# Second buffers and other PSUM banks behind the experts, and another order of loads and folds at the start, in a two-layer vision-text kernel

## The chip, the cores and the metric

One core of a Trainium2 chip runs the whole program, all of it in float32. The metric is the time of one execution on the device in microseconds; several executions of a kernel are timed, and their median is its time.

## The reference, cut to what matters

16 samples of 96 tokens (64 image patches and 32 text tokens) of 192 features pass through a patch embedding and two layers.

```python
x: (16, 3, 128, 128)   txt: (16, 32, 192)
# 1. patch tokens: the image and four shifted copies, cut into 16x16 patches (3840 values),
#    normalised and projected; folded here into 768 inner + 192 halo values a patch
tn = (t - mu) * rsqrt(var + 1e-05) * ln_weight + ln_bias
tok = einsum('bnk,dk->bnd', tn, proj_weight) + proj_bias
h = concatenate([tok, txt], 1)                        # (16, 96, 192)
# 2. layer 0: attention over 4 segments of 24 tokens, 12 heads; then top-2 of 8 experts
h += attention0(layernorm(h))
h += moe(layernorm(h))        # capacity 60 slots a pair group, F = 768, relu
# 3. layer 1: linear attention with L1-normalised q and k
q, k, v = split(layernorm(h) @ w_qkv.T)
q, k = q / sum_n |q|, k / sum_n |k|                   # over the tokens of a sample
h += (q @ (k^T @ v by head of 16)) @ w_proj.T + b_proj
# 4. layer 1: soft mixture, 8 experts x 4 slots
logits = l2norm(layernorm(h)) @ (scale * l2norm(slots))
xs = softmax(logits, over tokens)^T @ x ; y = expert_mlp(xs) with gelu
h += softmax(logits, over slots) @ y
```

## The kernel before

**Tiling.** The 1536 tokens lie in J = 4 tiles j of four samples. A tile is `h[:, j]`: 128 partitions (32 tokens of each of the four samples) by NB = 3 blocks by 192 features; blocks 0 and 1 are image tokens, block 2 is text. Every engine has its own program, written out by hand as a list of calls at the end of its block (TensorE lines 887 to 1142, ScalarE 1309 to 1450, VectorE 1900 to 2081, GpSimd 418 to 477, SyncE 294 to 349). Semaphores named in `wait_ge`, `need` and `free` tie them together; what stands behind a waiting call on the same engine waits too. PSUM has eight banks of 512 float32 a partition, given out by hand in constants (`TOK_AT`, lines 77 to 80) and by number inside the functions.

**Start.** SyncE issues all early loads (294 to 325): layernorm weights, the projection weights in four chunks (`load_weights`, 31 tiles of 128 x 192), the constants, images as eight pairs (`load_images`, 271: 448 KB of inner values and 32 KB of halo on 64 partitions, into NX = 6 places), the text tokens, then the weights of the first attention (316 to 323) and last images 4 to 7. VectorE folds the 31 weight tiles into KT = 8 tiles `w_eff` (`fold_weights`, 1463): for tile t a multiplication and up to four multiply-adds into the same destination, each of which waits for the one before it through `then` (1458); `head_values` (1547) later waits for the attention's weights. TensorE sums bias and columns (`weight_sums`, 499; the first WIDE_TILES = 15 bias matmuls are 128 columns wide, the others 32 wide on four column groups in turn) and multiplies patches (`patch_tile`, 490: four matmuls of 32 rows out, one for each sample; tile t = 7 has only 64 rows of contraction). `patches(2, 0)` (542, called at 896) waits for images 4 and 5. `scores(0)` (622) writes banks 5 to 7. ScalarE squares each image pair (`squares`, 1150); squares of images 6 and 7 (1318, 1319) stand ahead of `keep_inputs(0)` (1322), which copies the turned inputs that `reduce_inputs(0)` (595) needs. VectorE's `token_rows` (1492) reads what a patch matmul left.

**Experts.** `expert_inner` and `expert_outer` (702, 724) are a run of matmuls from 129 to 260 us. For the tiles j = 2 and 3, GpSimd gathers the experts' rows from DRAM (`fetch_row`, 446: 12 gathers) between its powers for the layernorms (`norm_scale`, 413), and VectorE adds them (`add_rows`, 1758); for j = 0 and 1 TensorE combines them (`combine`, 746; `add_experts`, 1749).

**Behind the experts** each tile passes through these steps. `linear_norm` (1775, VectorE) writes `xn`; `turn_linear` (764, TensorE) turns it with `flip` (246) into banks 0 and 1: 96 of its features would fill 96 rows twice, so it takes 128 features and 64 features instead, and the 64 are turned to two places so that the matmuls of 64 rows can use either half of the array. `linear_queries` (785) has two full matmuls and two of 64 rows, one on each half; `linear_keys_values` (774) writes banks 2 to 4, one full and one 64-row matmul a block, those of blocks 0 and 1 on different halves. ScalarE copies (`keep_linear_inputs` 1258, `keep_keys_values` 1264, `keep_linear_queries` 1271, `keep_linear_outputs` 1276). `key_products` (795) multiplies k and v into banks 1 to 4; `own_heads` (1811, VectorE) masks the product; `key_sums` (806), `key_norms` (1780), `query_norms` (1787), `norm_products` (1795) and `scale_queries` (1804) make the L1 norms; `linear_outputs` (813) and `linear_project` (823) end the attention, `add_linear` (1818) adds it. The soft layer follows: `soft_moments` and `soft_norm` (1827, 1834), `turn_soft`, `soft_logits`, `soft_max`, `slot_weights` (1858), `soft_inputs` (854, TensorE, bank 7), `keep_slots`, and for three tiles together and the last alone `soft_hidden` (862), `gelu_slots` (1303), `keep_own` (1880), then `slot_outputs` (870), `add_up_bias`, `token_outputs` (877) and `add_soft` (1892). One buffer each of `xn`, `xs`, `xsT`, `o1T`, `dsp_bd`, `mv_b`, `rs_b`, `mv_s` and `soft_st` serves all tiles.

```python
            def linear_queries(j):
                pe.wait_ge(sem("b_xnT"), j + 1)
                for mh in range(2):
                    nc.tensor.matmul(PS[0:HD, mh, 0:TOK], w_q1[:, 0, mh * HD:(mh + 1) * HD], xnT[:, 0], start=True, stop=False)
                for mh in range(2):
                    rows = slice(mh * DT, (mh + 1) * DT)
                    mm = nc.tensor.matmul(PS[0:HD, mh, 0:TOK], w_q1[rows, 1, mh * HD:(mh + 1) * HD], xnT[rows, 1],
                                          start=False, stop=True)
```

## Time and profile before

| | |
|---|---|
| median of 3 runs | 366.97 us (364.63 to 372.05) |
| profiled execution | 366.12 us, of which the span of instructions is 364.0 us |
| mean granted TensorE clock | 0.986 of full speed |
| busy, share of the span | TensorE 325.9 us (90%), VectorE 195.5 (54%), ScalarE 112.1 (31%), GpSimd 52.1 (14%) |
| HBM traffic | 19.94 MB read, 2.75 MB written |

The span runs from the first to the last instruction; 2.1 us of the execution lie around it. A float32 matmul shows in the trace as two matmul instructions, so "x4" in a row stands for two matmuls. Busy times of TensorE are modelled at their ends and overlap a little. "Released by" or "<-" names what ended a wait. The granted clock is 1.00 at TensorE's full clock (2.4 GHz) and half of that at the lower level (1.2 GHz).

### The profile page before, as it was taken

The numbers are of one execution on the slowest core, as the hardware profiler recorded it, in microseconds if no ns is written. First come the engines' busy times: TensorE is split into PE (matmuls) and PEld (weight loads), VectorE is DVE, ScalarE is ACT, GpSimd is POOL, SyncE is SP. The second block draws the span as 40 slices with busy tenths as digits, with TensorE's granted clock in tenths as the row PEclk, the third lists the DMA queues.
The fourth block names the chain that finished last, engine by engine and source line by source line (L and its number), as shares of the span: only waits on it lengthen the run. The fifth ranks groups of instructions, "written<-read, shape, count | busy, mean of one in ns | idle before, by whom it ended". The sixth has DMA issues, their size and how long they took to land.

```text
span 364.0 us, 9315 instructions
## 1 busy us (share of the span) xinstructions
PE 325.9 (90%) x3978; PEld 216.6 (60%) x3978; DVE 195.5 (54%) x636; ACT 112.1 (31%) x218; POOL 52.1 (14%) x99
## 2 busy tenths in 40 slices
PE   4898999887788989999999999999987899997765
PEld 3675567655665337475656657475854556666455
DVE  2925497899999971142312111120367655968655
ACT  1224444665642431404041221203012213333140
POOL 8403222100011000000010000000087201100100
PEclk9999999999999999999999999999999989999889
DMA  7936011332030000504132240000012000000005
GB/s 266 346 85 220 2 38 31 117 125 96 19 105 1 2 0 2 151 17 137 50 103 74 81 137 16 23 2 22 24 54 67 13 0 0 3 2 2 0 0 130
DMA packets 15876, 23.29 MB, mean 64 GB/s; under 512 B 3770, under 2 KB 11932, under 8 KB 15836
## 3 DMA queue, kind: packets, MB, share of 16 engines
q1 hardware_dynamic: 14364, 20.93, 18.4%
q0 software_dynamic: 576, 1.18, 1.2%
q10 hardware_dynamic: 896, 0.59, 0.7%
q8 instruction: 31, 0.51, 0.6%
q14 instruction: 9, 0.07, 0.1%
HBM read 19.94 MB, written 2.75 MB: 62 GB/s over the span
## 4 chain that ended last, share of the span: by engine, by line
PE 61%; DVE 20%; SPq 7%; issue 4%; DMA 3%; POOL 2%; ACT 2%; DVEq 0%; POOLq 0%; ACTq 0%
PE banks L719 18%; PE banks L734 17%; SPq L320 4%; PE banks L496 3%; PE banks L249 3%; PE banks L778 2%; PE banks L858 2%; DVE sb_onehot_combT L1695 2%; PE banks L820 2%; PE banks L830 2%; PE banks L788 2%; DMA sb_tok_xeT<-in_xhalo 2%; DVE sb_stat L1517 1%; POOL sb_onehot_combT L455 1%; PE banks L782 1%
## 5 line engine op out<-in xcount | busy, mean ns | idle before, releaser
L719 PE MATMUL banks<-sb_tok_xeT,sb_wi_sl 128*128 128x480 f32 (+1 forms) x192 | 64.9, 590 | 1.1 <-ACT sb_tok_xeT L1236 1.1
L734 PE MATMUL banks<-sb_wo_sl,sb_attn_hidT_attn 128*60 128x192 f32 x768 | 64.1, 327 | 0.0
L734 PEld LDWEIGHTS banks<-sb_wo_sl,sb_attn_hidT_attn 128*60 128x60 f32 x768 | 52.9, 133 | 12.4 <-issue 4.0
L1251 ACT ACTIVATE sb_attn_hidT_attn<-banks 128x480 f32<-128x480 f32 x48 | 25.6, 569 | 95.7 <-PE banks L719 95.7
L719 PEld LDWEIGHTS banks<-sb_tok_xeT,sb_wi_sl 128*128 128x128 f32 (+1 forms) x192 | 24.9, 187 | 37.7 <-issue 35.8
L1743 DVE COPY sb_w_tok_e_out<-banks 60x384 f32<-60x384 f32 x16 | 8.9, 555 | 61.9 <-PE banks L734 61.6
L496 PE MATMUL banks<-sb_tok_xeT 128*32 128x193 f32 (+1 forms) x512 | 24.7, 328 | 1.5 <-DMA sb_tok_xeT<-in_xhalo 1.5
L496 PEld LDWEIGHTS banks<-sb_tok_xeT 128*32 128x32 f32 (+1 forms) x512 | 17.2, 109 | 7.2 <-issue 4.5
L1745 DVE COPY sb_onehot_combT<-banks 60x384 f32<-60x384 f32 x16 | 8.9, 555 | 22.1 <-PE banks L734 22.0
L618 PE MATMUL banks<-sb_w_v,sb_xrT 97*32 97x96 f32 x512 | 13.7, 249 | 1.8 <-issue 1.2
L1155 ACT ACTIVATE sb_onehot_combT<-sb_tok_xeT 128x1024 f32<-128x1024 f32 x8 | 8.5, 1058 | 19.3 <-DMA sb_tok_xeT<-in_xhalo 19.0
L1517 DVE BATCH_NORM_STATS2 sb_stat<-sb_h 128x6 f32<-128x192 f32 x48 | 14.1, 348 | 0.5
L858 PE MATMUL banks<-sb_attn_hidT_attn 128*96 128x128 f32 x48 | 8.8, 353 | 5.7 <-DVE sb_attn_hidT_attn L1865 5.7
L618 PEld LDWEIGHTS banks<-sb_w_v,sb_xrT 97*32 97x32 f32 x512 | 10.8, 110 | 5.2 <-issue 2.1
L455 POOL DMA_INDIRECT sb_onehot_combT<-expert_rows,sb_row_of x12 | 12.1, 1011 | 6.6 <-DMA expert_rows<-sb_onehot_combT 3.4
L508 PE MATMUL banks<-sb_w_tok_e_out,sb_ln_b 128*128 128x192 f32 x30 | 7.7, 421 | 5.2 <-DMA sb_w_tok_e_out<-in_wtok 5.2
L443 POOL TENSOR_TENSOR sb_soft_stat<-sb_soft_stat,sb_half 128x6 f32<-128x6 f32 x4 | 5.3, 1337 | 47.4 <-DVE sb_soft_stat L1832 47.4
L1730 DVE TENSOR_TENSOR sb_comb<-sb_cst,sb_slot_of 128x480 f32<-128x480 f32 x6 | 3.9, 654 | 15.0 <-PE banks L249 15.0
L778 PE MATMUL banks<-sb_w_kv,sb_xnT 128*128 128x384 f32 x24 | 9.9, 520 | 1.9 <-DVE sb_attn_hidT_attn L1815 1.6
L858 PEld LDWEIGHTS banks<-sb_attn_hidT_attn 128*96 128x96 f32 x48 | 7.7, 221 | 6.4 <-DVE sb_attn_hidT_attn L1865 6.4
L438 POOL MEMSET sb_attn_hidT_attn<- 1x384 f32 x1 | 0.4, 412 | 77.0 <-PE banks L734 77.0
L249 PE MATMUL banks<-sb_cst,sb_attn_hidT_attn 128*128 128x128 f32 (+1 forms) x72 | 10.4, 278 | 0.7 <-DVE sb_attn_hidT_attn L1577 0.7
(252 smaller groups left out, 537.6 us busy)
## 6 DMA issues: line engine op xcount, KB each, us to landing
sb_wo_sl<-in_wo SPq DMA_DIRECT2D x8, 576.0 KB, 4.5
sb_tok_xeT<-in_xin SPq DMA_DIRECT2D x8, 448.0 KB, 5.4
sb_wi_sl<-in_wi SPq DMA_DIRECT2D x8, 288.0 KB, 3.0
sb_wi_sl<-in_wi SPq DMA_DIRECT2D x24, 96.0 KB, 3.0
sb_w_tok_e_out<-in_wtok SPq DMA_DIRECT2D x2, 960.0 KB, 7.5
expert_rows<-sb_onehot_combT SPq DMA_DIRECT2D x8, 192.0 KB, 4.2
sb_w_tok_e_out<-in_wtok SPq DMA_DIRECT2D x1, 576.0 KB, 9.5
out<-sb_h SPq DMA_DIRECT2D x8, 72.0 KB, 2.0
```

Source lines behind the costliest of these rows:

```text
L249: return nc.tensor.transpose(dst, src, ident[0:rows, 0:rows])
L320: sp.dma_start(dst, src).then_inc(sem("attn0_in"), 16)
L455: gp.indirect_dma_start(rows_in[:, i], None, expert_rows, bass.IndirectOffsetOnAxis(ap=row_of[:, i:i + 1], axis=0)).then_inc(sem(f"rows_in ...
L496: nc.tensor.matmul(PS[QB * b:QB * b + QB, bank, at:at + D + 1], x_k[0:rows, (2 * j + b // 2) % NX, t, cols], w_eff[0:rows, t], start=(t == ...
L618: mm = nc.tensor.matmul(PS[32 * r:32 * r + 32, V_BANK[b % 2], s * C1:(s + 1) * C1], xrT[:, at:at + 32], w_v4[:, r], start=True, stop=True)
L719: mm = nc.tensor.matmul(PS[:, banks[z], 0:SLOTS], lhs, rhs.rearrange("k g c -> k (g c)"), start=first, stop=not first)
L734: mm = nc.tensor.matmul(PS[64 * z:64 * z + CAP, 4 + hf, pr * D:(pr + 1) * D], hidT[:, e % 2, f, g * CAP:(g + 1) * CAP], wo_sl[:, q, f], st ...
L778: nc.tensor.matmul(PS[:, 2 + blk, 0:2 * D], xnT[:, 0, blk * 128:(blk + 1) * 128], w_kv1[:, 0], start=True, stop=False)
L858: mm = nc.tensor.matmul(PS[0:HD, 7, dh * 128:(dh + 1) * 128], xs[:, blk, dh * HD:(dh + 1) * HD], dsp_bd[:, blk].rearrange("t q s -> t (q s ...
L1251: nc.scalar.activation(hidT[:, e % 2, f], PS[:, HID_BANKS[(e * (FT // 2) + f // 2) % 2][f % 2], 0:SLOTS], ACT.Relu).then_inc(sem("hidT"), 1)
L1517: ve.bn_stats(stat6[:, blk], h[:, j, blk]).then_inc(sem("stat6"), 1)
L1743: ve.tensor_copy(e_out[64 * (e % 2):64 * (e % 2) + CAP, z:z + 3:2, e // 2], src).then_inc(sem("e_out"), 1)
```

## The change

*The start.* The constants are loaded in two parts, the 136 columns that the first work needs early and the rest behind the projection weights. Images 4 and 5 are loaded ahead of the text tokens and the attention's weights. The halo of every image is loaded twice, onto partitions 0 to 63 and 64 to 127; so are the last weight tile and two columns of `ln_w`. With them the last patch tile (t = 7) of the two blocks is done as eight matmuls one after another, block 0 on the upper and block 1 on the lower rows, for j = 0, 1, 2 (`PAIRED`). VectorE folds in the groups `FOLDS` = (0), (1, 2), (3, 4), (5, 6, 7), one shift of each tile in turn. TensorE works in three `STAGES`; WIDE_TILES is 20. Patch tiles of j = 1 and 2 write two banks each, (6, 7) and (4, 5), and `scores(0)` waits for `tok_mid` and `tok_var` of 6 instead of 4.

*Behind the experts.* `xn`, `xs`, `xsT`, `o1T`, `dsp_bd` and the small statistics have a second buffer, in `x_space` or beside the first. `xnT` holds 96 rows twice; `features` is gone, `w_q1` and `w_kv1` hold 96 rows, and layer 1 has 9 loads instead of 15. Queries are four matmuls of 96 rows, keys and values two a block, turning six transposes. Banks are named in constants. The lists of calls of all engines from `combine` on have a new order.

```diff
-WIDE_TILES = 15
+WIDE_TILES = 20
-LAYER1_DMAS = 15
+LAYER1_DMAS = 9
-TOK_AT = (((4, 0), (5, 0)), ((6, 0), (6, 200)), ((4, 0), (4, 200)), ((4, 0), (4, 200)))
+TOK_AT = (((4, 0), (5, 0)), ((6, 0), (7, 0)), ((4, 0), (5, 0)), ((4, 0), (4, 200)))
+FOLDS = ((0,), (1, 2), (3, 4), (5, 6, 7))
+STAGES = (((0, 1, 2), 25), ((3, 4), 25), ((5, 6), W_TILES))
+PAIRED = 3
+COMB_BANKS = ((0, 3), (3, 4))
+LIN_T_BANKS, LIN_Q_BANKS, LIN_KV_BANKS = (0, 1), (1, 3), (1, 0, 4)
+PROD_BANK, SUM_BANK, LIN_O_BANKS, PROJ_BANKS = 4, 0, (1, 2), (3, 2)
+SOFT_T_BANKS, SOFT_LOG_BANK, SOFT_IN_BANK, SOFT_HID_BANKS = (6, 4), 5, 2, (0, 1)
+SLOT_Y_BANKS, TOKEN_Y_BANKS = (6, 3), ((2, 6), (1, 0))
@@ SyncE
-                sp.dma_start(x_k[0:HALO2, q, KT - 1], xhalo[n]).then_inc(sem(f"x_in{q}"), 16)
+                for z in range(2):
+                    sp.dma_start(x_k[HALO2 * z:HALO2 * z + HALO2, q, KT - 1], xhalo[n]).then_inc(sem(f"x_in{q}"), 16)
-            sp.dma_start(cst[:], consts).then_inc(sem("cst_in"), 16)
+            sp.dma_start(cst[:, 0:FIRST_W], consts[:, 0:FIRST_W]).then_inc(sem("ones_in"), 16)
...
+            sp.dma_start(cst[:, FIRST_W:], consts[:, FIRST_W:]).then_inc(sem("cst_in"), 16)
             load_images(2)
             load_images(3)
+            load_images(4)
+            load_images(5)
             sp.dma_start(h[:, :, 2], txt.rearrange("(j b) t d -> (b t) j d", j=J)).then_inc(sem("txt_in"), 16)
...
-            for n in range(4, 8):
+            for n in range(6, 8):
                 load_images(n)
@@ GpSimd
             fetch_row(2, 2, 0)
-            norm_scale("b", 1, rs_b[:], mv_b)
             fetch_row(2, 2, 1)
+            norm_scale("b", 1, rs_b[:, 1], mv_b[:, 1])
             fetch_row(3, 0, 0)
             fetch_row(3, 0, 1)
             fetch_row(3, 1, 0)
+            norm_scale("b", 2, rs_b[:, 0], mv_b[:, 0])
             fetch_row(3, 1, 1)
@@ TensorE
+                if j < PAIRED and blk == 1:
+                    for both in range(2):
+                        patch_tile(j, both, KT - 1)
...
             def linear_queries(j):
                 pe.wait_ge(sem("b_xnT"), j + 1)
                 for mh in range(2):
-                    nc.tensor.matmul(PS[0:HD, mh, 0:TOK], w_q1[:, 0, mh * HD:(mh + 1) * HD], xnT[:, 0], start=True, stop=False)
-                for mh in range(2):
-                    rows = slice(mh * DT, (mh + 1) * DT)
-                    mm = nc.tensor.matmul(PS[0:HD, mh, 0:TOK], w_q1[rows, 1, mh * HD:(mh + 1) * HD], xnT[rows, 1],
-                                          start=False, stop=True)
+                    for kh in range(2):
+                        mm = nc.tensor.matmul(PS[0:HD, LIN_Q_BANKS[mh], 0:TOK], w_q1[:, kh, mh * HD:(mh + 1) * HD], xnT[:, kh],
+                                              start=(kh == 0), stop=(kh == 1))
...
-            free(tok_mid=4, tok_var=4)
+            free(tok_mid=6, tok_var=6)
             scores(0)
-            free(tok_mid=6, tok_var=6)
...
             combine(0, 0)
             combine(0, 1)
+            free(moe_h=2)
             combine(1, 0)
             combine(1, 1)
             turn_linear(0)
             free(b_xnT=1)
+            linear_keys_values(0, 0)
+            linear_keys_values(0, 1)
+            free(b_kv=1, moe_h=3)
             linear_queries(0)
-            linear_keys_values(0, (0, 1))
             free(moe_h=4)
-            linear_keys_values(0, (2,))
-            free(b_q1T=1)
+            linear_keys_values(0, 2)
+            free(b_kv=2, b_q1T=1)
             turn_linear(1)
-            free(b_kv=3, b_xnT=2)
+            free(b_kv=3)
             key_products(0)
+            free(b_xnT=2)
             key_sums(0)
-            free(b_kvbd=1)
-            linear_keys_values(1, (0, 1))
-            linear_keys_values(1, (2,))
+            linear_keys_values(1, 0)
+            free(b_knorm=1)
+            linear_keys_values(1, 1)
             free(b_kv=4)
             linear_outputs(0)
-            free(b_kv=6, b_o1T=1)
+            linear_keys_values(1, 2)
+            free(b_o1T=1)
+            linear_queries(1)
+            free(b_kv=6)
             key_products(1)
...
+            token_outputs(1)
+            free(y_added=2)
             slot_outputs(2)
@@ VectorE, fold_weights
+                for tiles in FOLDS:
+                    for s, t in [(s, t) for s in range(5) for t in tiles if s < len(shifts[t])]:
...
+                        if s == 0:
+                            ins = ve.tensor_scalar(dst, src, scale, None, ALU.mult)
+                        else:
+                            ve.wait_ge(sem("w_fold"), at[t])
+                            ins = ve.scalar_tensor_tensor(dst, src, scale, dst, ALU.mult, ALU.add)
@@ VectorE, the list near its end
+            token_weights(1)
             soft_max(2)
             token_shift(2)
-            add_linear(3, 1)
+            soft_norm(3)
             slot_weights(2)
-            soft_moments(3)
             token_weights(2)
-            soft_norm(3)
             soft_max(3)
```

## Rows read from the trace of the kernel before

**Rows 1.** Busy time by stage: us, each engine's busy (x instructions), clock, DMA share, GB/s.
```profile
0.00:50.00 50.00, 41.44 (x794) 29.68 (x797) 26.79 (x89) 16.90 (x25) 19.47 (x56) 1.00 0.50 168
50.00:268.00 218.00, 207.41 (x2564) 133.48 (x2556) 104.87 (x326) 69.85 (x141) 14.04 (x24) 1.00 0.19 58
268.00:290.00 22.00, 17.70 (x170) 10.36 (x170) 16.22 (x52) 5.87 (x10) 13.25 (x16) 1.00 0.17 46
290.00:331.00 41.00, 36.90 (x309) 24.52 (x310) 27.82 (x101) 11.82 (x24) 4.03 (x3) 0.96 0.00 1
331.00:361.00 30.00, 22.49 (x152) 18.56 (x150) 19.80 (x72) 7.68 (x19) 1.32 (x1) 0.89 0.09 23
```

**Rows 2.** Timeline of TensorE, first 50 us: start us, us, instruction, [idle before].
```profile
12.47 1.89 PE L508 MATMUL banks<-sb_w_tok_e_out,sb_ln_b 128*128 128x192 f32 x10
...
16.13 0.35 PE L523 MATMUL banks<-sb_tok_xeT,sb_cst 128*32 128x192 f32 x1 [1.00 <-DVE sb_tok_xeT L1476]
...
22.48 3.86 PE L496 MATMUL banks<-sb_tok_xeT 64*32 64x193 f32 x78
...
33.59 2.96 PE L496 MATMUL banks<-sb_tok_xeT 128*32 128x193 f32 x64 [1.51 <-DMA sb_tok_xeT<-in_xhalo]
...
46.57 1.32 PE L630 MATMUL banks<-sb_attn_hidT_attn,sb_qT 32*32 32x96 f32 x96 [0.37 <-ACT sb_attn_hidT_attn L1198]
```

**Rows 3.** Timeline of VectorE, first 50 us: folds, and instructions that don't wait.
```profile
10.18 1.79 DVE L1476 SCALAR_TENSOR_TENSOR sb_tok_xeT<-sb_w_tok_e_out,sb_ln_w,sb_tok_xeT 128x192 f32<-128x192 f32 x4
...
29.15 0.41 DVE L1500 SCALAR_TENSOR_TENSOR sb_tok_mid<-sb_col_sum,sb_tok_stat,banks 128x192 f32<-128x192 f32 x1
29.48 0.15 DVE L1503 SCALAR_TENSOR_TENSOR sb_tok_stat<-banks,sb_tok_stat 128x1 f32<-128x1 f32 x1
```

**Rows 4.** Timeline of SyncE's queue (DMA issues), first 60 us.
```profile
15.66 7.47 SPq L320 DMA_DIRECT2D sb_w_px<-in_wproj  x1
...
25.10 0.85 SPq L322 DMA_DIRECT2D sb_w_qkv<-in_bqkv  x1
```

**Rows 5.** Groups by line on TensorE, 268 to 331: busy us, mean ns | idle before.
```profile
L778 PE MATMUL banks<-sb_w_kv,sb_xnT 128*128 128x384 f32 x24 | 9.9, 520 | 1.9 <-DVE sb_attn_hidT_attn L1815 1.6 <-ACT sb_xnT L1262 0.3
L788 PE MATMUL banks<-sb_xnT,sb_w_q 128*96 128x384 f32 x16 | 7.4, 591 | 2.1 <-ACT sb_xnT L1262 1.0 <-DVE sb_attn_hidT_attn L1815 0.6 <-ACT sb_attn_hidT_attn L1279 0.4
...
L801 PE MATMUL banks<-sb_attn_hidT_attn 32*96 32x96 f32 x192 | 5.1, 249 | 1.9 <-issue 1.9
```

**Rows 6.** The chain that ended last, 265 to 364: one piece of it.
```profile
273.01 4.02 DMA sb_onehot_combT<-expert_rows,sb_row_of
```

**Rows 7.** Timeline of ScalarE, first 50 us.
```profile
35.87 1.06 ACT L1155 ACTIVATE sb_onehot_combT<-sb_tok_xeT 128x1024 f32<-128x1024 f32 x1
37.70 0.79 ACT L1173 COPY sb_xnT<-banks 96x768 f32<-96x768 f32 x1 [0.77 <-PE banks L249]
```

**Rows 8.** Timeline of TensorE, 260 to 364.
```profile
270.38 1.50 PE L788 MATMUL banks<-sb_xnT,sb_w_q 128*96 128x384 f32 x4 [1.03 <-ACT sb_xnT L1262]
...
272.63 1.56 PE L778 MATMUL banks<-sb_w_kv,sb_xnT 128*128 128x384 f32 x4
274.12 0.92 PE L782 MATMUL banks<-sb_w_kv,sb_xnT 64*128 64x384 f32 x4
...
276.65 1.20 PE L249 MATMUL banks<-sb_cst,sb_xn 128*128 128x128 f32 x9
...
285.47 1.60 PE L820 MATMUL banks<-sb_attn_hidT_attn 96*96 96x96 f32 x16
...
290.34 2.87 PE L788 MATMUL banks<-sb_xnT,sb_w_q 128*96 128x384 f32 x4 [0.63 <-DVE sb_attn_hidT_attn L1815]
...
330.73 1.57 PE L820 MATMUL banks<-sb_attn_hidT_attn 96*96 96x96 f32 x16 [0.90 <-DVE sb_attn_hidT_attn L1809]
...
348.87 2.88 PE L858 MATMUL banks<-sb_attn_hidT_attn 128*96 128x128 f32 x12 [2.43 <-DVE sb_attn_hidT_attn L1865]
```

**Rows 9.** Timeline of VectorE, 258 to 364: its last instruction.
```profile
360.31 0.35 DVE L1898 TENSOR_TENSOR sb_h<-sb_h,banks 128x192 f32<-128x192 f32 x1
```

446 lines of the change are left out of this document (224 added, 222 removed).

## The prediction

> **What bounds the kernel now.** I read the stages first [rows 1]: the reader is to see that TensorE is busy 207 of 218 us between 50 and 268, and that the time it loses lies in the first 50 us (41.4 busy) and behind the experts: 17.7 of 22, then 36.9 of 41 with the granted clock at 0.96, then 22.5 of 30 at 0.89. VectorE is busy 64 of these last 93 us, so no engine is full there. The change touches only those two ends. Then the start, engine by engine. TensorE waits 1.00 us for a folded weight tile, runs densely from 16.1, and stands idle 1.51 us ahead of the patches of images 4 and 5 [rows 2]. The folds come 0.445 us apart (four in 1.79, each of them 0.42 long and 0.03 of hand-over), though VectorE starts an instruction that doesn't wait 0.33 us after the one in front, 29.15 to 29.48 [rows 3]. SyncE issues the loads of images 4 to 7 late because one small load held it 7.47 us [rows 4]. Last, the layer behind the experts, where the groups of matmuls name the waits [rows 5]: 8.7 us of idle time from 268 to 331 over the view's twelve groups (the three with most of it are shown), behind ScalarE's copies and VectorE's masked products. A part of it hangs on a gather that takes 4.02 us to land [rows 6], behind which VectorE's queue stands.
>
> **The start.** The constants are cut in two and the first weights therefore come some 0.5 us earlier (an estimate: 220 of 288 KB no longer stand ahead of them). *Folds in turns.* 24 dependent folds at 0.445; with a fold of another tile between, the wait is met before it is reached. I take 0.33 a fold for the eight of each pair and 0.445 for the last tile's four: tiles 1 and 2 done near 12.0, 3 and 4 near 15.8, all near 19.0 instead of 20.6. *TensorE.* Five more bias matmuls are 128 columns wide and no longer run four abreast: ten instructions take 1.89 us [rows 2], about 1.4 us more than narrow ones. Against that it needs no fold before it has done 25 bias tiles, so it runs without a gap from 5.25: bias tiles to 15.4, patch tiles 0 to 2 to 17.9, 3 and 4 to 19.5, 5 and 6 to 21.7. *Last tile side by side.* Eight matmuls of 64 rows use both halves of the array at once: 0.37 us saved for each of three pairs, worth 1.1 us in all (0 if they don't run together). The 78 instructions that end at 26.3 [rows 2] thus end near 24.9: 1.4 us gained. *Images moved up.* Images 4 and 5 then land near 23, far ahead of the need at 30.7, so the 1.51 us go and patches(2, 0) ends about 3.2 us earlier.
> What is late next is SyncE's queue. The attention weights are issued behind six more image DMAs, and wherever the queue fills up the 7.47 us come again, now from a later point. By the order of the queue I put the last weight's issue at 29.8 (25.1 to 25.95 before) and its landing near 33; head_values and first_norm(0) wait a few tenths. ScalarE must square images 6 and 7 before it may copy the turned inputs; image 7's square began at 35.87 and the copy at 37.70 [rows 7]. Image 7 was last in the queue before and still is; two images instead of four share the way, so I take 35.3 to 36.3 for its landing and 37.4 for the copy's start at the latest. reduce_inputs(0) comes at 38.0 instead of 40.4: 2.4 us gained. One new wait takes some back: patch tiles of j=2 now lie in banks 4 and 5, so scores(0) waits for VectorE's token rows of tile 5, some 0.4 us beyond the ScalarE copy that released it at 46.57 [rows 2]; behind it in TensorE's queue stand all values(0, ·), and VectorE's score_max waits for it. **The start gains 2.0 us less hops: 1.8.** From there on the attention is a chain over VectorE and TensorE that nothing in the diff touches, and the experts are pure matmul [rows 1], so I carry 1.8 through unchanged. Bounds: 3.2 if only the images count; for the other end see the SyncE rival.
>
> **The layer behind the experts: what it costs TensorE.** The 64-row halves that ran side by side are given up. Queries: two full matmuls (1.50) and two halves together, 2.25 us from 270.38 to 272.63; now four full ones at 0.75, 3.05. Keys and values: 4.02 us from 272.63 to 276.65; now six full ones, 4.6. Turning: six transposes instead of nine (1.20 for nine), about 0.3 us less [rows 8]. Net +1.05 us a tile (0.8 + 0.6 - 0.35), **+4.2 us for four tiles**. The Trainium skill says the same against this edit (TensorEngine Tiling (Array Packing), Key Properties and Theoretical Speedup): tiles on different rows execute in parallel, up to twice as fast with a contraction of 64. The trace agrees, 0.92 us for a pair of 64-row matmuls against 1.56 for two full ones [rows 8]. By a clean factor of two the price would be 1.5 - 0.35 a tile, 4.6 us, and the sum 359.2.
>
> **And what it frees.** combine(1, 0) reuses bank 3 and waits for add_experts(0, 1), 0.4 us. The turned inputs and q, kv no longer share banks 0 and 1 with each other's readers, the four product banks lie apart from kv (4 to 7, against 1 to 4), xn, xs, xsT, o1T, the slot weights and the moments have second buffers, and the kv and query matmuls stand where TensorE waited for VectorE. I walked the three queues with the durations of this trace. Per tile TensorE then has 0.7 turning, 4.6 kv, 3.05 queries, 1.25 products, 0.1 sums, 1.5 outputs, 2.1 projection: 13.3 us, plus 2 to 3.3 us of the soft layer from the third tile on. Starts of linear_outputs: 283.1, 296.4, 310.9, 323.8, against 285.47 (first) to 330.73 (fourth) [rows 8]. Up to there 2.4 us of idle time are left of the 8.7, and the queries at half clock (2.87 against 1.50) become warm, because TensorE has no gap ahead of them; one soft_inputs (1.3) has moved behind. 6.9 us gained there. The gather costs less than it did: POOL issues (2, 2, 1) ahead of the second pow, 1.1 us earlier, but (3, 1, 1) and on now stand behind norm_scale of tile 2; VectorE waits about 0.8 us for them at a place where TensorE has work.
> Behind that comes latency. In VectorE's queue soft_norm(3) stands in front of slot_weights(2), which makes soft_inputs(2) start at 336.2, and soft_logits(3) queues behind it. I keep half clock for the 336 to 343 stretch, as at 348.87 (2.88 for twelve instructions). soft_inputs(3) starts near 343 instead of 348.87, the closing slot and token matmuls take about 0.5 us more (slot_outputs(2) now waits for two additions). Last addition 353.4 instead of 360.3 to 360.7 [rows 9]: 7.3 us. A walk leaves out hand-overs of 0.05 us between engines; for some 35 of them I take 1.8 us off. **The layer gains 5.5 us.** Bounds of this part: minus 4.2 (only the dearer matmuls, no wait gone) and plus 11 (all 8.7 idle, all cold surplus of 331 to 361 gone, less 4.2 and the tail's latency).
>
> **Sum.** 366.12 (profiled execution, span 364.0, 2.1 us around it) - 1.8 - 5.5 = 358.8. The three runs shown had their median at 366.97, 0.85 above the profiled one and within their own scatter of 7 us; I forecast 358.8. A measurement of this kernel tells about 2% from no change, that is 7.3 us: a median under 359.6 is faster.
>
> **Rivals.**
> *Waits only change places.* In-order VectorE still decides in 268 to 331 (27.8 of 41 busy, and each long copy comes with a semaphore hop), so filling matmuls only lengthen the queue ahead of the urgent ones. For it: ScalarE and VectorE idle little when TensorE does. Against: the idle time stands before banks that the change splits. Of 6.9 gained, 4.2 + 1.5 are lost: 366.12 - 1.8 - 0 to 1.5 = 363.5. Chance 0.22.
> *TensorE stays warm to the end.* The half-clock rows of 338 to 352 become full-clock: two soft_inputs 1.4 us less each, the hidden matmuls 1.4, and fewer hops than I took off: 366.12 - 1.8 - 10 = 354.3. For it: the new order has the last soft matmuls close together. Against: 4 to 5 us of idle time ahead of them remain in my walk. Chance 0.17.
> *SyncE pays twice (slower side).* The place is the issue of w_px behind the small packets of v_mask. If it stalls behind the images' queue as well as behind v_mask, another 7.5 us, image 7 lands at 43.4 and its square ends at 44.5; the input copy starts there, 6.8 us later than at 37.70. It decides from the moment that square ends after about 39.5, and with 5.5 gained behind the experts the sum is 366.12 + 6.8 + 0.4 - 5.5 = 367.8; with the first rival too, 371. Chance 0.07.
> *Folds gain nothing.* If VectorE's next instruction can't start before the pipe is empty, folds in turns still come 0.445 apart; all are done at 20.4, and TensorE waits 0.9 us: 359.7. Chance 0.06. The Trainium skill states this (VectorE: DVE Perf Modes, The DRAIN you can't avoid): a semaphore after each operation costs nothing extra. The trace does not agree, 0.33 against 0.445.
> The forecast itself has 0.48, with 356.5 to 361.5 as its own range.
>
> **Chances.** Faster by over 2%: all of the warm case, two thirds of my own, little of the folds: 0.52. Within 2%: 0.42. Slower: 0.06, mostly a stall larger than the one priced. Range 353 to 366: the warm case's middle is inside, the first rival too, the double stall is left out.
>
> **What would show it.** Right: no idle time before the patches of images 4 and 5; folds 0.33 apart; queries of 3.0 us and kv of 1.5 a block; four linear_outputs starts 13 to 14.5 us apart, the first about 4 us, the fourth about 8 to 9 us earlier than now; clock 1.00 in 290 to 300. Wrong: ScalarE's copy of the turned inputs after 38, an idle TensorE over 4 us in 268 to 331, or a clock above 0.95 in the last 30 us.

## The result: 352.6 us, 13 us less than before

The changed kernel takes 352.63 us (median of 4 executions, 350.76 to 353.82) against 365.80 for the kernel before beside it (364.00 to 372.05): ratio 0.965, 95% interval 0.960 to 0.970. The forecast was 358.8 with a range from 353 to 366; the result lies 0.4 us below the range. The direction was right, the size was not: the medians differ by 13.2 us. Between the profiled executions, on which the sum was made, it is 366.12 to 351.75, 14.4 us where 7.3 were forecast. The span is 349.9.

First the stages, to be laid beside [rows 1]. The limits are set at the same places of the program: until the experts' results are being combined, until some 5 us behind the first linear_outputs, until the fourth one, until the last addition. Columns: stretch and its length, busy time of TensorE, its weight loads, VectorE, ScalarE and GpSimd (with instructions), TensorE's granted clock, DMA share, GB/s.

```profile
0.00:50.00 50.00, 42.15 (x850) 30.72 (x850) 26.79 (x95) 18.25 (x28) 18.97 (x56) 1.00 0.57 179
50.00:265.00 215.00, 204.09 (x2496) 131.16 (x2494) 101.89 (x319) 68.49 (x137) 14.27 (x24) 1.00 0.20 57
265.00:285.00 20.00, 18.18 (x131) 11.46 (x126) 16.33 (x52) 6.04 (x10) 13.15 (x17) 1.00 0.19 50
285.00:318.00 33.00, 32.61 (x335) 24.33 (x334) 26.58 (x93) 11.01 (x21) 4.07 (x4) 1.00 0.01 2
318.00:347.00 29.00, 22.45 (x164) 18.94 (x164) 22.02 (x81) 8.68 (x22) 1.90 (x2) 0.94 0.09 24
```

The reader is to see where the gain lies: the third and fourth stretch last 53 us together instead of 63, and TensorE's idle time in them is 2.2 us (53 less 18.18 and 32.61) instead of 8.4. In the last stretch little changed; it is still a quarter idle.

The timeline of TensorE over one tile of the layer, to be laid beside [rows 8] (start us, length us, instruction, count, idle time before it and what ended it):

```profile
265.76 0.86 PE L264 MATMUL banks<-sb_cst,sb_xn 128*96 128x128 f32 x6
267.65 2.82 PE L810 MATMUL banks<-sb_w_kv,sb_xnT 96*128 96x384 f32 x8 [1.03 <-ACT sb_xnT L1290]
270.30 2.74 PE L818 MATMUL banks<-sb_xnT,sb_w_q 96*96 96x384 f32 x8
272.88 1.45 PE L810 MATMUL banks<-sb_w_kv,sb_xnT 96*128 96x384 f32 x4
...
280.21 1.57 PE L847 MATMUL banks<-sb_attn_hidT_attn 96*96 96x96 f32 x16
...
292.42 1.52 PE L847 MATMUL banks<-sb_attn_hidT_attn 96*96 96x96 f32 x16
...
305.90 1.52 PE L847 MATMUL banks<-sb_attn_hidT_attn 96*96 96x96 f32 x16
...
318.02 1.57 PE L847 MATMUL banks<-sb_attn_hidT_attn 96*96 96x96 f32 x16 [0.40 <-DVE sb_attn_hidT_attn L1843]
```

Queries are the eight instructions of L818: from their start to that of the next group, 270.30 to 272.88, it is 2.6 us. Keys and values are the x8 and the x4 of L810, 2.65 and 1.3 us by their starts, 3.95 together. The forecast had 3.05 and 4.6. The four linear_outputs (L847) stand 12.2, 13.5 and 12.1 us apart, where the walk had 13.3, 14.5 and 12.9: about one microsecond less in each. Counted from the start of combine (257.18 now, 259.81 before), the fourth starts at 60.8 instead of 70.9.

At the start, beside [rows 2, 4 and 7], on TensorE, SyncE's queue and ScalarE:

```profile
12.88 1.89 PE L530 MATMUL banks<-sb_w_tok_e_out,sb_ln_b 128*128 128x192 f32 x10 [0.33 <-DMA sb_w_tok_e_out<-in_wtok]
...
37.85 1.51 PE L634 MATMUL banks<-sb_xnT,sb_w_red 96*104 96x384 f32 x4 [0.89 <-ACT sb_xnT L1201]
...
44.44 1.32 PE L666 MATMUL banks<-sb_attn_hidT_attn,sb_qT 32*32 32x96 f32 x96 [0.83 <-DVE sb_tok_stat L1537]
```

```profile
23.32 3.48 SPq L340 DMA_DIRECT2D sb_w_px<-in_wproj  x1
...
28.00 0.85 SPq L342 DMA_DIRECT2D sb_w_qkv<-in_bqkv  x1
```

```profile
35.97 1.06 ACT L1183 ACTIVATE sb_onehot_combT<-sb_tok_xeT 128x1024 f32<-128x1024 f32 x1 [1.02 <-DMA sb_tok_xeT<-in_xhalo]
36.93 0.77 ACT L1201 COPY sb_xnT<-banks 96x768 f32<-96x768 f32 x1
```

The idle time ahead of the patches of images 4 and 5 is gone, SyncE's stall is 3.48 us instead of 7.47, and scores(0) starts at 44.44 instead of 46.57: 2.1 us, forecast 2.0. (Whether the edits earn these 2.1 us is another question; further executions of the old start, below, reach the same place without them.) The last image's square is now directly ahead of the copy, which waits for nothing else.

### The profile page after: what moved, and what is told of

Read it like the earlier page. It is cut to its first block, busy times and chain, and to the rows that moved or that the text cites. A ratio compares the mean times of both kernels' runs of the same rounds, so it can differ in the third digit from the quotient of the medians.

```text
span 349.9 us, 9294 instructions
## 1 busy us (share of the span) xinstructions
PE 319.5 (91%) x3966; PEld 216.6 (62%) x3966; DVE 193.6 (55%) x636; ACT 112.5 (32%) x218; POOL 52.4 (15%) x100
## 4 chain that ended last, share of the span: by engine, by line
PE 64%; DVE 16%; SPq 8%; issue 4%; DMA 3%; POOL 2%; ACT 2%; DVEq 0%; POOLq 0%
PE banks L755 18%; PE banks L770 18%; PE banks L810 3%; PE banks L264 3%; SPq L288 2%; PE banks L818 2%; SPq L340 2%; PE banks L654 2%; PE banks L857 2%; PE banks L847 2%; PE banks L522 2%; DVE sb_onehot_combT L1729 2%; DVE sb_stat L1551 2%; POOL sb_onehot_combT L478 2%; SPq L286 1%
## 5 line engine op out<-in xcount | busy, mean ns | idle before, releaser
L522 PE MATMUL banks<-sb_tok_xeT 128*32 128x193 f32 (+1 forms) x512 | 23.4, 328 | 0.0
L522 PEld LDWEIGHTS banks<-sb_tok_xeT 128*32 128x32 f32 (+1 forms) x512 | 15.8, 109 | 5.9 <-issue 2.3
L810 PE MATMUL banks<-sb_w_kv,sb_xnT 96*128 96x384 f32 x48 | 17.6, 497 | 1.0 <-ACT sb_xnT L1290 1.0
L1551 DVE BATCH_NORM_STATS2 sb_stat<-sb_h 128x6 f32<-128x192 f32 x48 | 14.1, 349 | 0.6
L530 PE MATMUL banks<-sb_w_tok_e_out,sb_ln_b 128*128 128x192 f32 x40 | 8.9, 385 | 5.8 <-DMA sb_w_tok_e_out<-in_wtok 5.8
L478 POOL DMA_INDIRECT sb_onehot_combT<-expert_rows,sb_row_of x12 | 12.3, 1025 | 6.0 <-issue 3.0
L530 PEld LDWEIGHTS banks<-sb_w_tok_e_out,sb_ln_b 128*128 128x128 f32 x40 | 7.9, 225 | 6.6 <-issue 5.4
L810 PEld LDWEIGHTS banks<-sb_w_kv,sb_xnT 96*128 96x128 f32 x48 | 8.5, 190 | 5.4 <-ACT sb_xnT L1290 1.3
L818 PE MATMUL banks<-sb_xnT,sb_w_q 96*96 96x384 f32 x32 | 11.0, 486 | 0.0
L717 PE MATMUL banks<-sb_onehot_combT,sb_xn 64*128 64x480 f32 x48 | 10.7, 578 | 0.2 <-issue 0.2
```

What stands on the lines that cost most here:

```text
L478: gp.indirect_dma_start(rows_in[:, i], None, expert_rows, bass.IndirectOffsetOnAxis(ap=row_of[:, i:i + 1], axis=0)).then_inc(sem(f"rows_in ...
L522: nc.tensor.matmul(PS[QB * b:QB * b + QB, bank, at:at + D + 1], x_k[rows, (2 * j + b // 2) % NX, t, cols], w_eff[rows, t], start=(t == 0), ...
L530: nc.tensor.matmul(PS[:, 0, 0:D], ln_b[:, k:k + 1].to_broadcast([128, 128]), w_tok[:, k], start=(k == 0), stop=False)
L717: mm = nc.tensor.matmul(PS[:, banks[hf], 0:E * CAP], xn2[rows, j, blk, 0:128], onehot[rows, j % 2, blk], start=(blk == 0), stop=(blk == NB ...
L810: mm = nc.tensor.matmul(PS[:, LIN_KV_BANKS[blk], 0:2 * D], xnT[:, kh, blk * 128:(blk + 1) * 128], w_kv1[:, kh], start=(kh == 0), stop=(kh ...
L818: mm = nc.tensor.matmul(PS[0:HD, LIN_Q_BANKS[mh], 0:TOK], w_q1[:, kh, mh * HD:(mh + 1) * HD], xnT[:, kh], start=(kh == 0), stop=(kh == 1))
```

## The experiments

Sixteen kernels ran in four groups, each group beside the kernel before on the same chip (the second and the fourth group on one chip, the others on two more). That kernel's median moved with the chip: 365.1, 371.2, 366.5 and 371.8 us. So times of different groups are compared by their ratio to it only. The last four columns are places in the one profiled execution of each kernel: the starts of scores(0) and of combine, and, counted from the start of combine, the starts of the fourth linear_outputs ("LO4") and of the last addition ("end").

| kernel | median us | ratio to before (95%) | scores(0) | combine | LO4 | end |
|---|---|---|---|---|---|---|
| before | 365.80 | 1 | 46.57 | 259.81 | 70.9 | 100.5 |
| after | 352.63 | 0.965 (0.960 to 0.970) | 44.44 | 257.18 | 60.8 | 89.1 |
| b_full96 | 364.94 | 0.997 (0.992 to 1.002) | 44.39 | 257.45 | 72.7 | 103.5 |
| b_twobuf | 368.48 | 1.012 (1.005 to 1.020) | 45.91 | 259.38 | 69.4 | 99.6 |
| b_start | 364.40 | 1.001 (0.998 to 1.004) | 45.83 | 262.64 | 69.2 | 99.1 |
| a_halves | 359.70 | 0.986 (0.978 to 0.993) | 45.26 | 261.55 | 63.7 | 94.8 |
| a_bench | (one execution, with matmuls added behind its work) | | 44.52 | 257.70 | 60.1 | 91.1 |
| a_again | 355.81 | 0.966 (0.955 to 0.978) | 46.64 | 260.29 | 61.1 | 90.1 |
| a_imgback | 356.19 | 0.964 (0.948 to 0.981) | 46.45 | 259.99 | 60.1 | 91.4 |
| a_foldseq | 355.05 | 0.963 (0.952 to 0.975) | 44.38 | 258.24 | 61.0 | 92.3 |
| a_nopair | 353.71 | 0.970 (0.964 to 0.975) | 45.07 | 258.37 | 60.1 | 87.8 |
| a_wide15 | 354.60 | 0.970 (0.965 to 0.975) | 44.00 | 257.67 | 60.1 | 91.4 |
| a_tail | 356.67 | 0.976 (0.972 to 0.981) | 44.69 | 258.13 | 60.8 | 90.5 |
| a_tailwide | 357.23 | 0.977 (0.972 to 0.982) | 45.27 | 258.00 | 60.1 | 93.5 |
| a_base | 357.89 | 0.969 (0.960 to 0.978) | 44.40 | 258.30 | 61.0 | 92.3 |
| b_both | 369.69 | 0.998 (0.992 to 1.004) | 45.07 | 258.47 | 75.4 | 107.5 |
| a_warm | 352.16 | 0.955 (0.948 to 0.962) | 44.24 | 259.95 | 60.2 | 87.1 |
| a_warm2 | 350.97 | 0.951 (0.945 to 0.958) | 44.54 | 258.49 | 60.1 | 87.0 |

### What the full matmuls cost

**b_full96** is the kernel before with only this edit:

```diff
-                    nc.tensor.matmul(PS[:, 2 + blk, 0:2 * D], xnT[:, 0, ...], w_kv1[:, 0], start=True, stop=False)
-                for blk in blks:
-                    rows = slice(blk % 2 * DT, (blk % 2 + 1) * DT)
-                    nc.tensor.matmul(..., xnT[rows, 1, ...], w_kv1[rows, 1], start=False, stop=True)
+                    for kh in range(2):
+                        nc.tensor.matmul(..., xnT[0:HD, kh, ...], w_kv1[:, kh], start=(kh == 0), stop=(kh == 1))
```

(the same for the queries, and six transposes a tile instead of nine).

> The kernel before with one edit: queries as four matmuls of 96 rows, keys and values as two of 96 rows a block, six transposes a tile; order, banks and buffers as before. The prediction's price (four full matmuls 3.05 us for 2.25, six full ones 4.6 for 4.02, less 0.35 for the transposes: +1.05 us a tile) says 2 to 4 us slower, since some of it falls into waits: ratio 1.005 to 1.011. The rival, that the rows of before are dear because TensorE changes between full and half-array matmuls (0.84 us for a single matmul there, 0.66 for one in the kernel after), says queries 2.65, keys and values 3.95, nothing dearer: 1 us faster to 0.5 slower, ratio 0.997 to 1.001.

Measured: no slower, ratio 0.997. Its LO4 is 1.8 us later than before; that lies between the first two linear_outputs (17.8 us apart instead of 16.3, with a clock of 0.77 in 285 to 300), and the next two distances, 15.0 and 14.4, are near those of before, 14.9 and 14.1. **a_halves** is the other way round, the changed kernel with 128-row and 64-row matmuls again.

> The kernel after with that one edit undone: 128 features and 64 features, the 64-row query matmuls side by side, nine transposes; order, banks and buffers as after. The prediction's price says 0.5 us a tile cheaper (queries 0.8, a half alone as dear as a full one, transposes 0.3 dearer): ratio to before about 0.959, 2 us under the kernel after. The rival says each change between full and half costs some 0.17 us, keys and values 5.0 us for 3.95, queries 0.4 less, transposes 0.3 more: 3 to 4 us over the kernel after, ratio 0.973 to 0.976.

Measured: 0.986 instead of 0.965 (of another group), slower where the forecast's price makes it faster, and by more than the rival said. **a_bench** shows why. It is the changed kernel with groups of 384-column matmuls behind its own work.

> The kernel after the change with a row of matmuls behind its own work, 384 columns wide each, in groups of their own: 24 to warm up, 12 of 128 rows, 12 of 96 rows, 12 of 64 rows on alternating halves, then the queries in the old form (two of 128 rows, two halves) and in the new one (four of 96 rows), four times each, then keys and values of one block in the old form (128, 128, 64, 64, 128, 64 rows) and in the new one (six of 96 rows), four times each. The time means nothing, the rows do. Theory of my prediction: a pair of halves costs 0.92 us against 1.56 for two full ones, so the old queries take 4 x 2.25 = 9.0 us and the new ones 12.2 us; keys and values 4 x 1.34 = 5.4 against 6.1 us. Rival (a switch between row sizes costs as much as the overlap saves): full matmuls of 96 rows cost the same as of 128, the halves alone run at half the pitch (about 0.17 us each at full clock), but each change between full and half adds 0.1 us or more, so that the old and new forms of each take the same time within 10%, and the old form of keys and values, with three changes a block, is the dearer one.

The timeline of TensorE behind the kernel's end (L1181 128 rows, L1184 96 rows, L1189 64 rows on alternating halves; one matmul is two instructions):

```profile
364.80 7.90 PE L1181 MATMUL banks<-sb_wo_sl,sb_wi_sl 128*96 128x384 f32 x24
372.54 7.91 PE L1184 MATMUL banks<-sb_wo_sl,sb_wi_sl 96*96 96x384 f32 x24
380.38 4.11 PE L1189 MATMUL banks<-sb_wo_sl,sb_wi_sl 64*96 64x384 f32 x24
384.42 1.53 PE L1181 MATMUL banks<-sb_wo_sl,sb_wi_sl 128*96 128x384 f32 x4
385.88 0.89 PE L1189 MATMUL banks<-sb_wo_sl,sb_wi_sl 64*96 64x384 f32 x4
386.70 1.53 PE L1181 MATMUL banks<-sb_wo_sl,sb_wi_sl 128*96 128x384 f32 x4
...
393.54 10.56 PE L1184 MATMUL banks<-sb_wo_sl,sb_wi_sl 96*96 96x384 f32 x32
...
407.85 1.56 PE L1181 MATMUL banks<-sb_wo_sl,sb_wi_sl 128*128 128x384 f32 x4
409.34 0.92 PE L1189 MATMUL banks<-sb_wo_sl,sb_wi_sl 64*128 64x384 f32 x4
410.19 0.91 PE L1181 MATMUL banks<-sb_wo_sl,sb_wi_sl 128*128 128x384 f32 x2
411.03 0.91 PE L1189 MATMUL banks<-sb_wo_sl,sb_wi_sl 64*128 64x384 f32 x2
411.87 1.56 PE L1181 MATMUL banks<-sb_wo_sl,sb_wi_sl 128*128 128x384 f32 x4
...
419.90 15.75 PE L1184 MATMUL banks<-sb_wo_sl,sb_wi_sl 96*128 96x384 f32 x48
```

The granted clock is 1.00 throughout. To be seen: a full instruction follows the one in front by 0.325 us whether it has 96 or 128 rows, a half one by 0.168 (24 in 4.04). The old queries repeat every 2.28 us (384.42 to 386.70), though four of each would be 1.97: two changes between full and half cost 0.31, about 0.15 each. The new ones are a quarter of 10.56 less the last one's tail, 2.6. The old keys and values repeat every 4.02 us (407.85 to 411.87) for twelve instructions, the new ones are 15.75 / 4 = 3.94. So the price per tile is +0.3 for the queries, -0.1 for keys and values, and -0.3 for three transposes fewer: nothing. The rival of this run is right. Where a lone full matmul stands between halves it takes 0.84 us instead of 0.65, and a lone half takes 0.84 too (410.19 to 411.87): the 64 rows save nothing.

So the 0.75 us of the forecast for a full matmul are right for the old form, where two of them (four instructions) stand ahead of a change: 1.46 us from 384.42 to 385.88, 1.49 in [rows 8] from 272.63 to 274.12. Four instructions in a run of their own kind take 4 x 0.325 = 1.30; the rest is mostly the change, which the new form does not make. The trace of the kernel before had such a run, where the forecast could have read it, in soft_hidden, eight instructions of 96 rows and 384 columns in 2.69 us, 0.67 a matmul:

```profile
341.35 2.86 PE L866 MATMUL banks<-sb_tok_xeT,sb_w_down 96*96 96x384 f32 x8 [0.46 <-ACT sb_tok_xeT L1300]
344.04 0.82 PE L249 MATMUL banks<-sb_cst,sb_attn_hidT_attn 128*96 128x128 f32 x6
```

In a_halves every block comes alone in the new order, the worst form. Its timeline:

```profile
272.36 0.88 PE L818 MATMUL banks<-sb_w_kv,sb_xnT 128*128 128x384 f32 x2 [1.04 <-ACT sb_xnT L1301]
273.17 0.91 PE L820 MATMUL banks<-sb_w_kv,sb_xnT 64*128 64x384 f32 x2
...
275.69 1.53 PE L826 MATMUL banks<-sb_xnT,sb_w_q 128*96 128x384 f32 x4
```

Two blocks take 3.33 us here (272.36 to 275.69) against 2.65 in the changed kernel, which makes 5.0 against 3.95 for three. With nine transposes for six (+0.3) and the queries (-0.3) that is 1.0 a tile. Its linear_outputs stand 13.2, 14.3 and 12.1 us apart instead of 12.2, 13.5 and 12.1, and LO4 is 2.8 us later. Only these 2.8 us can be put down to the halves. Its span is 10.0 us longer than the changed kernel's (359.9 against 349.9): 4.4 lie ahead of combine, where none of its matmuls differ, with a clock of 0.83 to 0.86 between 80 and 100, and 2.8 behind LO4, in half-clock time that most traces in the new order have as well (a_base 31.4 us from LO4 to the last addition, a_halves 31.1).

The Trainium skill's factor of two for two 64-row tiles (TensorEngine Tiling (Array Packing), Theoretical Speedup) agrees with the trace: 24 instructions in 4.11 us against 7.90. What decided here is the 0.15 to 0.19 us at each change between full and half.

### Buffers, banks and order

**b_twobuf** is the kernel before with the second buffers of xn, xs, xsT, o1T, the slot weights and the moments, in the old order and banks; **b_both** adds the full matmuls to it.

```diff
-        o1T = mid[0:HD + 1, 3264:4032]...
+        o1T = [... for x in (mid[0:HD + 1, 3264:4032], x_space[0:HD + 1, 5888:6656])]
...
-                need(ve, "b_xnT_ps", j)
+                need(ve, "b_xnT_ps", j - 1)
```

> The kernel before with the second buffers alone (xn, xs, xsT, o1T, the slot weights, the moments and their powers), order, banks and matmuls untouched. Theory A, the order of the queues binds and the buffers only allow another order: 0 to 1 us faster, ratio 0.997 to 1.000. Theory B, the buffers' own waits were the idle time: 4 us and more, ratio 0.989 or less.

> The kernel before with the second buffers and with the full 96-row matmuls, in the old order and the old banks. Theory A (order and banks bring the gain): like each of the two alone, the same as before within 1%, fourth linear_outputs 69 to 72 us behind combine's start (before 70.9, after 60.8). Rival (the two needed each other, because the buffers only help once keys and values are single full blocks): 65 us or less, and a ratio to before of 0.985 or lower.

Measured: 1.012 and 0.998. Under the old order neither buffers nor matmuls nor both bring anything; LO4 stays at 69 to 75. The 75.4 of b_both is outside both forecasts, which had 69 to 72 and 65 or less. Two stretches of it, around its first two linear_outputs (290.06 and 304.56):

```profile
278.00:298.00 20.00, 15.79 (x114) 10.30 (x107) 8.26 (x23) 2.52 (x5) 4.16 (x6) 0.74 0.06 16
298.00:318.00 20.00, 18.53 (x153) 13.57 (x152) 14.97 (x56) 7.18 (x14) 2.70 (x2) 1.00 0.00 1
```

TensorE still waits, and in this execution that cost it the clock too (0.74). Its first linear_outputs comes 31.6 us behind combine, where the other kernels in the old order have 25.3 to 25.7; from there its distances are the usual ones. These distances are the cleanest sign. In the old order the last three linear_outputs stand 14.9 to 15.0 and 14.1 to 14.4 us apart, with any buffers and any form of the matmuls; in the new order it is 13.5 and 12.1 (14.3 and 12.1 with the halves). Theory A holds: the gain behind the experts comes with the new order and banks together, the buffers being part of that bundle. How it divides between order and banks stays open, as does whether the new order needs the second buffers: no run has one without the others.

### The start, part by part

**b_start** is the kernel before with the whole new start.

> The kernel before with the whole start of the kernel after (constants cut, images 4 and 5 moved up, halo twice, folds in turns, stages, last patch tile side by side, banks of the patches) and the layer behind the experts untouched. The prediction said 1.8 us; the trace of the kernel after has its combine matmuls 2.6 us earlier. If the two ends only add up: 2.1 to 2.8 us faster, ratio 0.992 to 0.995. If the layer behind the experts takes something back (gathers landing at another time): under 1.5 us.

Measured: 1.001, no gain, where even the lower of its two forecasts had one. In its profiled execution scores(0) stands at 45.83, 0.7 us earlier than in the kernel before, the clock between 50 and 150 us is 0.93 to 0.94 (before 1.00), and combine starts 2.8 us later than in the kernel before.

The old start was traced four times: before, b_full96, b_twobuf and b_both have it unedited. Its scores(0) lies at 46.57, 44.39, 45.91 and 45.07, its combine between 257.45 and 259.81. In b_full96 TensorE waits neither for a fold nor for an image once it has its first weights (in [rows 2] 1.00 and 1.51 us), and ScalarE's copy of the turned inputs starts at 35.51, earlier than the changed kernel's 36.93:

```profile
28.46 5.83 PE L496 MATMUL banks<-sb_tok_xeT 128*32 128x193 f32 x128
...
44.39 1.31 PE L630 MATMUL banks<-sb_attn_hidT_attn,sb_qT 32*32 32x96 f32 x96 [0.38 <-ACT sb_attn_hidT_attn L1193]
```

The nine traces with the whole new start (after, b_start, a_halves, a_bench, a_again, a_tail, a_base and the two a_warm) have scores(0) at 44.24 to 46.64, median 44.5, against 45.5 for the old, and combine at 257.18 to 262.64, median 258.5, against 258.9. So of the 2.1 us at scores(0) between the first two profiled executions 1.0 is left between the medians, and of the 2.6 us at combine 0.4, both inside the scatter; and the waits that the new start was to remove come and go in the old one. A gain of the start is not shown. The parts were tried from the changed kernel's side. **a_again** is the changed kernel unedited.

> The kernel after the change once more. What is asked is how far its time and its clock move between executions: 350.8 to 353.8 us so far, clock 0.995 with 1.00 between 50 and 250 us. Theory 'the clock is part of the gain': some executions show stretches of 10 us at under 0.9 between 60 and 115 us, as the kernels with the old start or the old halves did, and are 2 to 4 us longer. Theory 'the new order keeps it warm': all lie within 1.5 us of each other and every stretch of the attention has a clock of 0.98 or more.

Measured: ratio 0.966, the four within 1.7 us of each other, and a clock of 0.84 in 110 to 120 in the profiled one. So the new order does not keep the attention warm, and the first theory is the nearer.

**a_imgback** takes the two images back down SyncE's list, **a_foldseq** folds each tile by itself, **a_nopair** runs the last tile's blocks one behind the other, **a_wide15** has 15 wide bias tiles:

```diff
-            load_images(4)
-            load_images(5)
...
-            for n in range(6, 8):
+            for n in range(4, 8):
```

```diff
-FOLDS = ((0,), (1, 2), (3, 4), (5, 6, 7))
+FOLDS = ((0,), (1,), (2,), (3,), (4,), (5,), (6,), (7,))
```

```diff
-PAIRED = 3
+PAIRED = 0
...
-WIDE_TILES = 20
+WIDE_TILES = 15
```

(the last block is two kernels, one line each).

> After, with the loads of images 4 and 5 back behind the attention weights; all else stays. My prediction: the 1.5 us idle time ahead of the patches of images 4 and 5 is back, ScalarE's copy of the turned inputs comes back towards 37.7 to 38.5, scores(0) 1 to 1.6 us later than 44.4, time 352.6 + 1.0 to 1.6 = 354. Rival (SyncE's queue only shifts its stall): image 7 lands no later than in the changed kernel, because four images behind the small packets instead of two ahead and two behind leave its place in the queue as it is; the copy stays at 36.9 and the time at 352.6 within 0.5.

> After, with each weight tile folded by itself (its four dependent steps one behind the other) instead of two or three tiles in turns; all else stays. My prediction: the folds come 0.445 us apart instead of 0.34, the last ends near 20.6 instead of 18.7, TensorE waits about 0.9 us more in its first stages, and scores(0) comes 0.9 later: 353.5. Rival (folds are covered by what TensorE does ahead of them, and by the images and copies behind): folds end later but scores(0) moves less than 0.3 us, time 352.6.

> After, with the last patch tile's two 64-row blocks one behind the other again (the constant PAIRED from 3 to 0); all else stays. My prediction gave the side-by-side form 0.37 us for each of three image pairs. Theory 'they overlap and it counts': TensorE's stretches of that tile take 0.37 us more, and of the three only those ahead of the turned inputs can show: scores(0) 0.4 to 0.7 us later after the first patches, time +0.7. Rival (the token rows are waited for elsewhere): the matmuls run longer but scores(0), counted from the end of the first patches, moves less than 0.2 us. The times themselves will hardly tell it, because the arrival of the second weight chunk alone moved 3 us between executions.

> After, with 15 instead of 20 bias tiles in the wide form (128 columns); all else stays. My prediction charged the five wide tiles 1.4 us. Theory 'TensorE sets the first 15 us': the 50 bias matmuls end 1.4 us earlier, the fold of tile 3 or the first images become the wait, and 0.5 to 1.4 us are left at scores(0): 351.5. Rival (loads and folds set it): TensorE waits longer for the second or third weight chunk or for the folds in exactly that measure, scores(0) moves less than 0.3 us against an execution with the same chunk arrival.

None of the four differs from the changed kernel by its time. Their traces say more, from TensorE's timelines. a_again and a_imgback had the second weight chunk late:

```profile
10.99 6.69 PE L530 MATMUL banks<-sb_w_tok_e_out,sb_ln_b 128*128 128x192 f32 x30 [2.04 <-DMA sb_w_tok_e_out<-in_wtok]
```

```profile
10.19 6.97 PE L528 MATMUL banks<-sb_w_tok_e_out,sb_ln_b 128*128 128x192 f32 x30 [1.25 <-DMA sb_w_tok_e_out<-in_wtok]
...
33.59 2.51 PE L520 MATMUL banks<-sb_tok_xeT 128*32 128x193 f32 x56 [0.91 <-DMA sb_tok_xeT<-in_xhalo]
```

The first is the changed kernel itself: with a chunk 2.04 us late its scores(0) comes at 46.64, 2.2 us later than in a_base, which doesn't wait for the chunk. Where the chunk comes in time, the last image decides: reduce_inputs (L634) waits for the copy behind its square and starts at 37.85, and at 37.80 with folds one by one, although those made TensorE wait 0.33 us more. So the start is the later of two paths. Where the last image decides, folds in turns are covered (scores(0) at 44.38 without them, 44.44 and 44.40 with them). Where TensorE's path decides, the moved images are worth 0.3 us, although a 0.91 us wait comes back without them: from the first narrow bias matmul to scores(0) 29.03 us in a_again, 29.36 in a_imgback. The pair is worth 0.9 there: 29.93 in a_nopair, in which L634 waits for nothing. Fifteen wide tiles end the bias matmuls earlier, and then the images are waited for, 0.21 and 1.07 us; 0.4 us are left at scores(0). What these parts are worth is thus up to 0.9 us in single traces, less than the 2 us by which the place of scores(0) moves from one execution to the next.

### The tail and the clock

**a_tail** moves one line up on TensorE:

```diff
-            free(s_xtT=2)
-            soft_inputs(2)
             free(s_dexp=3, s_lgT=3)
             soft_logits(3)
+            free(s_xtT=2)
+            soft_inputs(2)
```

> After, with the logits of the last soft tile ahead of soft_inputs(2) on TensorE. In the changed kernel TensorE stands idle 3.19 us for VectorE's soft_norm(3), then runs soft_inputs(2) at half clock (2.84), and the logits come behind it at 333.08; VectorE waits 1.96 us for them. Theory 'TensorE is full from there on': logits at 330.3, VectorE's wait goes, but soft_hidden(0, 3) holds TensorE until 336.3 as before, so soft_inputs(3) and the end move less than 0.5 us. Rival (the logits are on the path): end 1 to 1.5 us earlier.

Measured: 0.976, and 2 to 3 us slower than its neighbours a_nopair and a_wide15 on the same chip, which neither theory had. Its timeline:

```profile
329.25 1.51 PE L264 MATMUL banks<-sb_cst,sb_tok_xeT 128*96 128x128 f32 x6 [3.19 <-DVE sb_tok_xeT L1559]
331.80 0.87 PE L877 MATMUL banks<-sb_tok_xeT,sb_slot_n 96*32 96x96 f32 x16 [1.03 <-ACT sb_tok_xeT L1313]
332.59 2.88 PE L885 MATMUL banks<-sb_attn_hidT_attn 128*96 128x128 f32 x12
336.02 2.82 PE L893 MATMUL banks<-sb_tok_xeT,sb_w_down 96*96 96x384 f32 x8 [0.55 <-ACT sb_tok_xeT L1328]
```

soft_inputs(2) used to run while ScalarE copied the turned tile. Now TensorE waits 1.03 us for that copy with nothing to do, and soft_hidden waits 0.55 us for its input. From the last turn_soft to the last token_outputs it is 17.0 us here, 15.6 in the changed kernel's first profiled execution and 16.4 in a_again, where the turning too ran at half clock; so part of the loss is argued from this wait and part may be clock. **a_tailwide** has 15 wide tiles too.

> The two edits together (15 wide bias tiles, last logits ahead of soft_inputs(2)), tried as a version that could beat the changed kernel. Where both help: 352.6 - 1.0 - 1.0 = 350.6. Where the loads and the full TensorE decide: the same time as the changed kernel within 0.5 us, counted on the same chip.

It is the same as a_tail, 0.977, and not the 350.6 us of the hope.

Of the four rows the first three run at half clock, behind 3.19 us of idle time. **a_warm** puts matmuls that nobody reads into that gap, **a_warm2** one more into the next:

```diff
+            def keep_warm(n):
+                for _ in range(n):
+                    nc.tensor.matmul(PS[0:HD, 7, 0:384], w_down[:, 0, 0:HD], w_kv1[:, 0], start=True, stop=True)
...
             soft_logits(2)
+            keep_warm(4)
             turn_soft(3)
+            keep_warm(1)
```

(the last line in a_warm2 only), with **a_base**, the changed kernel, beside them.

> The kernel after the change, as the base for the three beside it on this chip. 352 to 356 us by the executions so far; the place of the fourth linear_outputs at 60.1 to 61.1 us behind the start of combine, as in all its executions so far.

> After, with four extra 384-column matmuls (2.6 us, into an unused bank, read by nobody) in TensorE's idle 3.19 us between the logits of tile 2 and turn_soft(3); nothing else. Theory (the idle time cools TensorE and the cold rows are on the path): soft_inputs(2) takes 1.5 us instead of 2.84, the hidden matmuls 2.6 instead of 2.8, clock from 0.92 to 0.98 or more in that stretch, end 1.3 us earlier in the executions that were cold for 2 us and up to 3 us in those that were cold for longer, ratio to the changed kernel 0.992 to 0.996. Rival (the clock falls anyway, or VectorE paces the tail): the rows stay at half clock, or the next wait grows by what they lose; same time within 0.5 us.

> The same with one more such matmul (0.66 us) in the idle 0.95 us between turn_soft(3) and soft_inputs(2). Theory as for the kernel with four: another few tenths at most, and the last executions that are still cold become warm. Rival: it delays soft_inputs(2) where VectorE's weights come first, 0.1 to 0.3 us slower than with four.

TensorE's timeline of a_base and then of a_warm2:

```profile
329.59 1.00 PE L264 MATMUL banks<-sb_cst,sb_tok_xeT 128*96 128x128 f32 x6 [3.18 <-DVE sb_tok_xeT L1559]
331.54 2.85 PE L885 MATMUL banks<-sb_attn_hidT_attn 128*96 128x128 f32 x12 [0.95 <-DVE sb_attn_hidT_attn L1901]
...
335.12 5.43 PE L893 MATMUL banks<-sb_tok_xeT,sb_w_down 96*96 96x384 f32 x8
```

```profile
325.64 2.82 PE L916 MATMUL banks<-sb_w_kv,sb_w_down 96*96 96x384 f32 x8
...
329.73 0.81 PE L916 MATMUL banks<-sb_w_kv,sb_w_down 96*96 96x384 f32 x2
330.84 1.52 PE L885 MATMUL banks<-sb_attn_hidT_attn 128*96 128x128 f32 x12 [0.30 <-DVE sb_attn_hidT_attn L1907]
...
332.92 2.79 PE L893 MATMUL banks<-sb_tok_xeT,sb_w_down 96*96 96x384 f32 x8
```

By the windows the granted clock of the 15 us behind 332 is 0.70 in a_base and 1.00 in a_warm2. soft_inputs(2) takes 1.52 us instead of 2.85, soft_hidden 2.79 instead of 5.43, and the last token_outputs starts at 343.1 instead of 348.2. The six executions of a_warm2 lie from 350.1 to 354.1 us, those of a_warm from 351.0 to 355.2, the six of a_base on the same chip from 355.2 to 361.5; the medians differ by 6.9 and 5.7 us, the ratios to the kernel before are 0.951 and 0.955 against 0.969. a_base itself, forecast at 352 to 356, came out at 357.9. What the fillers give can be read behind LO4, from there to the last addition: 27.0 us in both kernels, 31.4 in a_base, 28.3 in the changed kernel's first profiled execution. So it is 4.4 us against a long half-clock stretch and 1.3 against a short one; of the medians' 5.7 and 6.9 us the part beyond 4.4 is not explained by them. The theory of these two runs is right and its size, at most 3 us, too small. The fifth matmul is not seen to do anything: with and without it soft_inputs(2) starts 12.3 us behind LO4. By median and ratio a_warm2 is the fastest kernel of this study, but not clearly faster than a_warm.

## Why the prediction was wrong in size

**The step that failed** is "Net +1.05 us a tile ..., +4.2 us for four tiles". It measured about 0 in a_bench. The 3.05 and the 4.6 took 0.75 to 0.77 us for a full matmul, from a group of two (1.50) that stands ahead of halves. Most of what this has above 0.65 is the price of the change from full to half, and the new form, which makes no change, was charged with it; the same changes are why the halves had saved so little. In the profiled execution 3.2 us of the 4.2 are seen up to the fourth linear_outputs: it stands 60.8 us behind combine where the walk has 64.0, with each of three distances 0.8 to 1.1 us shorter than walked, and the first linear_outputs 0.3 us sooner.

**The rest of the miss.** The two profiled executions differ by 7.0 us more than forecast. Besides these 3.2, 1.8 are the hand-overs, 0.9 lie behind the fourth linear_outputs, 0.8 ahead of combine, and 0.3 outside the span. That the walk's 7.3 with the term at 0 gives 11.5, next to the 11.4 measured from combine to the last addition, is partly luck: the 0.9 behind the fourth linear_outputs come from a half-clock stretch shorter than walked.

**The 1.8 us taken off for hand-overs** are seen in no row: up to the fourth linear_outputs, where the walk without hand-overs had 6.9 us, 10.1 were gained. In an execution like a_base's, whose tail has more half clock, the layer gained 8.2 us and not 11.4. The tail was forecast at half clock in 336 to 343; what happens there differs by up to 3.6 us between executions of the new order with an unedited tail (27.7 to 31.4 from LO4 to the last addition). How the 13 us between the medians divide over start, layer and clock is open. The layer's part is seen in every trace: 87.8 to 92.3 us from combine to the last addition in the changed kernel and its variants with an unedited layer, 99.1 and 100.5 in the two traces of the old layer.

**What was right.** The waits that go: 2.2 us of idle time left between the experts and the fourth linear_outputs, 2.4 forecast; the first linear_outputs 23.0 us behind combine, 23.3 walked. The queries behind the experts run at full clock (1.00 in 285 to 300, where before had 0.89). The start's number was met by luck: 2.1 us at scores(0) against 2.0, while b_full96 reaches the same place, 44.39, with the old start, and b_start is no faster than before. The step that carried 1.8 us of it unchanged to the end is not borne out. Of its mechanisms one is seen in VectorE's timeline, beside [rows 3]:

```profile
9.47 2.72 DVE L1511 SCALAR_TENSOR_TENSOR sb_tok_xeT<-sb_w_tok_e_out,sb_ln_w,sb_tok_xeT 128x192 f32<-128x192 f32 x8
```

Folds in turns come 0.33 us apart (eight of 0.42 in 2.72) against 0.445, so an instruction that waits for the one directly in front does pay here for what the Trainium skill calls free (VectorE: DVE Perf Modes, The DRAIN you can't avoid); it was only not on the path. The new wait of scores(0) for VectorE is there, 0.83 us where 0.37 stood for ScalarE. The three pairs of 64-row blocks: 0.9 us together where nothing covers them, 1.1 forecast.

**The rivals.** "Waits only change places" fell with the idle time and with LO4. "TensorE stays warm to the end" gave 354.3, nearest to what came, but for a reason that did not hold: the last 29 us had a clock of 0.94, and a_warm2 shows that the warm tail was still to be had. SyncE's second stall did not come; its one stall halved. "Folds gain nothing" is wrong in its mechanism (they do come closer), and yet they bring nothing, because the last image's square is later.

## What to carry to other kernels

Read the price of a matmul from start to start inside a run of its own kind, and look at the neighbours; that holds for this form, float32 with 384 columns: splitting a contraction into 128 and 64 rows saves only where several halves stand together, since each change of form costs 0.15 to 0.19 us; equal matmuls of 96 rows may be had for nothing and can be placed one at a time, which an order needs. Second buffers gave nothing by themselves: change the order that they allow in the same step and price them together. Before a gain of 2 us is put down to an edit, see where the unedited kernel's other executions stand. And where an engine stands idle ahead of the last, serial part, a few matmuls that nobody reads may give several microseconds more.

## What the runs showed of the hardware

- 96 and 128 rows take the same 0.325 us per instruction of 384 columns, 64 rows on alternating halves 0.168, and a lone half between full ones 0.42 (0.84 for two instructions), as much as a lone full one there.
- Around 3.2 us of idle time TensorE's granted clock went from 2.4 to 1.2 GHz in all three profiled executions of the changed kernel. Behind it soft_inputs(2) ran at half clock in the first of them (2.84 us against 1.50), and soft_hidden too in a_base's (5.43 against 2.79). With 2.8 us of matmuls in that gap (a_warm) both ran at full clock.
- The wait for the second weight chunk differed by 2 us between executions of the same program (none in a_base, 0.33 and 2.04 us in the two others), enough to hide every edit of the start.
